# Cross-attention with a feed-forward block: softmax denominators summed on 32 rows of each head and divided chunk by chunk

## The reference, cut to what matters

```python
q, k, v = hidden @ Wq, context @ Wk, context @ Wv      # hidden = layernorm(x)
q, k = layernorm(q, gq, bq), layernorm(k, gk, bk)      # per head of 32
scores = einsum('bhqd,bhkd->bhqk', q, k) / sqrt(32)
attn = softmax(scores, axis=-1)
x = x + einsum('bhqk,bhkd->bhqd', attn, v) @ Wo
s = layernorm(x) @ Win + bin_
h = relu(s[..., None] * W1 + b1)                       # 64 x 16 hidden values
x = x + ((einsum('btmh,mh->btm', h, W2) + b2) @ Wout + bout)
```

## Time and profile before

| | |
|---|---|
| median of three runs | 479.64 us |
| the profiled execution: its time, its span | 481.05 us, 479.2 us |
| busy: TensorE | 433.5 us, 90% |
| VectorE | 358.1 us, 75% |
| ScalarE | 331.6 us, 69% |
| GpSimd | 204.4 us, 43% |
| mean granted TensorE clock | 0.96 of full |
| chain that ended last: TensorE, VectorE, ScalarE | 69%, 15%, 5% |
| one round of the steady part (201.15 to 252.12) | 50.97 us |

### The profile page before, as it was taken

The page is one execution under the profiler, slowest core; times in us unless marked ns, Lnnn a source line. Parts: engine busy times, 40 slices in busy tenths (PEclk is TensorE's granted clock), DMA queues, the critical chain, the costliest instruction groups (busy, mean ns, idle before and its releaser), DMA issues.

```text
span 479.2 us, 7952 instructions
## 1 busy us (share of the span) xinstructions
PE 433.5 (90%) x2456; PEld 279.3 (58%) x2456; DVE 358.1 (75%) x742; ACT 331.6 (69%) x633; POOL 204.4 (43%) x189
## 2 busy tenths in 40 slices
PE   5699888999999999999999999999987998799924
PEld 2386656467376737675667647664653564357712
DVE  4799796687767996799678977695788637537885
ACT  3658747896828983798559856896479639653880
POOL 3326666345514551546253643276342502057300
PEclk9999989999999999999999999999996999799975
DMA  8552685771915187516941493119700690052004
GB/s 306 153 167 68 142 211 138 170 183 33 243 33 126 33 206 168 134 46 156 215 111 28 105 269 67 27 22 234 184 5 0 168 261 16 22 162 80 1 1 175
DMA packets 25290, 58.35 MB, mean 122 GB/s; under 512 B 5921, under 2 KB 6433, under 8 KB 22177
## 3 DMA queue, kind: packets, MB, share of 16 engines
q1 hardware_dynamic: 24992, 57.58, 45.7%
q10 hardware_dynamic: 256, 0.26, 0.2%
HBM read 22.18 MB, written 8.39 MB: 64 GB/s over the span
## 4 chain that ended last, share of the span: by engine, by line
PE 69%; DVE 15%; issue 5%; ACT 5%; SPq 4%; POOL 0%; DMA 0%; DVEq 0%; ACTq 0%; POOLq 0%
PE bank L1929 33%; PE bank L2028 8%; PE bank L1935 7%; PE bank L2016 6%; PE bank L1994 4%; DVE bank L841 4%; PE bank L2096 3%; DVE mx L769 2%; ACT hid L1433 2%; PE bank L2081 2%; PE bank L2031 2%; DVE ssq L757 2%; DVE ln L665 1%; PE bank L2040 1%; PE bank L2003 1%
## 5 line engine op out<-in xcount | busy, mean ns | idle before, releaser
L769 DVE TENSOR_REDUCE mx<-bank 128x4 f32<-128x512 f32 x128 | 83.1, 684 | 22.2 <-PE bank L1994 22.0
L1353 ACT ACTIVATE prob<-bank 128x512 f32<-128x512 f32 x128 | 72.3, 596 | 31.1 <-PE bank L2016 29.1
L520 POOL TENSOR_TENSOR qt_lo<-u,qt_hi 128x512 fp32r<-128x512 f32 x32 | 41.3, 1293 | 70.5 <-ACT u L1330 70.3
L1433 ACT ACTIVATE hid<-s_in,b_col,w_col 128x256 f32<-128x256 f32 x128 | 68.2, 597 | 1.9 <-DVE s_in L821 1.5
L2028 PE MATMUL bank<-prob,v_kv 128*32 128x512 f32 x256 | 66.8, 620 | 0.1
L2031 PE MATMUL bank<-prob,den_sel 128*32 128x512 f32 x256 | 66.3, 621 | 0.0
L841 DVE SCALAR_TENSOR_TENSOR bank<-hid,w_col,bank 128x256 f32<-128x256 f32 x120 | 58.1, 485 | 6.9
L1929 PE MATMUL bank<-wq_hi,zt_hi 128*128 128x512 f32 x128 | 55.3, 432 | 3.0 <-DVE wq_lo L683 3.0
L2016 PE MATMUL bank<-q_stack,k_stack 97*128 97x512 f32 x128 | 50.8, 446 | 7.0 <-DVE att L796 5.9
L513 POOL TENSOR_TENSOR u<-u,lnq 128x512 f32<-128x512 f32 x32 | 32.9, 1050 | 53.8 <-DVE lnq L670 53.8
L525 POOL TENSOR_TENSOR at_lo<-att,at_hi 128x512 fp32r<-128x512 f32 x28 | 35.4, 1281 | 39.3 <-ACT at_hi L1405 39.3
(11 more groups left out here) (158 smaller groups left out, 899.0 us busy)
## 6 DMA issues: line engine op xcount, KB each, us to landing
q_stack<-qt_hi SPq DMA_DIRECT2D x64, 256.0 KB, 4.9
xin<-in_x_dram SPq DMA_DIRECT2D x36, 256.0 KB, 3.9
q_stack<-qt_lo SPq DMA_DIRECT2D x32, 256.0 KB, 4.7
x<-in_x_dram SPq DMA_DIRECT2D x28, 256.0 KB, 4.7
out_dram<-x SPq DMA_DIRECT2D x28, 256.0 KB, 3.3
att<-in_L_xattn_Wk_dram SPq DMA_DIRECT2D x1, 1024.0 KB, 6.5
x<-in_L_xattn_Wq_dram SPq DMA_DIRECT2D x4, 256.0 KB, 7.4
hid<-in_L_xattn_Wv_dram SPq DMA_DIRECT2D x1, 1024.0 KB, 10.2
```

Source lines behind the costliest of these rows:

```text
L520: pool.tensor_tensor(qt_lo[:, :, cols], u[:, j, :].rearrange("p (i n) -> p i n", i=HC), qt_hi[:, :, cols].bitcast(F32), ALU.subtract).then ...
L769: dve.tensor_reduce(mx[:, j, :].rearrange("p (g i) -> p i g", g=G)[:, 2 * half:2 * half + 2, 2 * r:2 * r + 2], maxs_banks[T][half][j][r][: ...
L1353: act.activation(prob[:, h % PR, :], score_bank[t][h][:, :], ACT.Exp, scale=SCALE).then_inc(exp_done, 1)
L1433: act.activation(hid[:, hh % RR, :], of_half(s_in), ACT.Relu, bias=b1_col[:, hh:hh + 1], scale=w1_col[:, hh:hh + 1]).then_inc(hid_done, 1)
```

## The change: what it does

The denominators are summed with a tile of ones of 32 columns, so each head's sum comes out on all of its 32 rows at once, in one bank for each chunk. They are inverted and multiplied chunk by chunk; the spreading matmuls, the split of the inverse, the copy `move_att` and the selectors go. The ring of exponentials has 8 tiles, and `values` and `denominators` take a chunk of four heads each. The Newton step writes back to `rden`, which has two slots.

```diff
-PR = 4
+PR = 8
-        den_sel = sb("den_sel", [P, C, HD])
-        bc_sel = sb("bc_sel", [P, C, P], F32R)
+        ones = sb("ones", [P, HD])
-        rden = sb("rden", [P, TOK])
+        rden = sb("rden", [P, 2, TOK])
...
-            def rden_error(t):
-            def rden_fix(t):
-            def rden_split(t):
+            def rden_error(t, c):
+
+                dve.wait_ge(rden_act, t * C + c + 1)
+                dve.scalar_tensor_tensor(out=den_bank[t][c][:, :], in0=den_bank[t][c][:, :], scalar=-1.0,
+                                         in1=rden[:, c % 2, :], op0=ALU.mult, op1=ALU.mult).then_inc(rden_step, 1)
+
+            def rden_fix(t, c):
+
+                dve.wait_ge(rden_step, t * C + c + 1)
+                dve.scalar_tensor_tensor(out=rden[:, c % 2, :], in0=den_bank[t][c][:, :], scalar=2.0,
+                                         in1=rden[:, c % 2, :], op0=ALU.add, op1=ALU.mult).then_inc(rden_done, 1)
...
+                dve.tensor_tensor(att_of(T)[:, c, :], at_bank[T][c][:, :], rden[:, c % 2, :], ALU.mult).then_inc(att_done, 1)
...
-            def move_att(t, c):
-            def rden_ln(t):
-            def rden_guess(t):
-            def rden_high(t):
+            def rden_ln(t, c):
+
+                act.wait_ge(pv_done, t * PAIRS + 2 * c + 2)
+                if c >= 2 or not first(t):
+                    act.wait_ge(att_done, t * C + c - 1)
+                act.activation(rden[:, c % 2, :], den_bank[t][c][:, :], ACT.Ln).then_inc(rden_log, 1)
+
+            def rden_guess(t, c):
+                act.wait_ge(rden_log, t * C + c + 1)
+                act.activation(rden[:, c % 2, :], rden[:, c % 2, :], ACT.Exp, scale=-1.0).then_inc(rden_act, 1)
...
-            def values(t, pair):
-            def spread(T, c):
+            def values(t, c):
+
+                pe.wait_ge(exp_done, t * H + HC * (c + 1))
...
+                for i in range(HC):
+                    n = HC * c + i
+                    ins = pe.matmul(at_bank[t][c][HD * i:HD * (i + 1), :], v_kv[kv_of(t)][:, n * HD:(n + 1) * HD],
+                                    prob[:, n % PR, :], start=True, stop=True)
                 ins.then_inc(pv_done, 1)
...
+            def denominators(t, c):
+
+                for i in range(HC):
+                    ins = pe.matmul(den_bank[t][c][HD * i:HD * (i + 1), :], ones[:, :], prob[:, (HC * c + i) % PR, :],
+                                    start=True, stop=True)
+                ins.then_inc(pv_done, 1)
```

```diff
+                values(t - 1, 1)
...
+                    pe.wait_ge(out_done, t * 4 - 9)
+                denominators(t - 1, 1)
+                if t >= 3:
+                    pe.wait_ge(out_done, t * 4 - 8)
...
+                max_scores(t, 1, 1)
...
                 scores(t - 1, 8)
...
+                    pe.wait_ge(rden_done, t * 4 - 3)
...
+                max_scores(t, 0, 2)
+                pe.wait_ge(mx_done[1], t * 8 + 3)
                 scores(t - 1, 9)
-                pe.wait_ge(exp_done, t * 16 - 8)
+                pe.wait_ge(exp_done, t * 16 - 7)
                 scores(t - 1, 10)
...
+                pe.wait_ge(mx_done[1], t * 8 + 4)
                 scores(t - 1, 11)
...
+                pe.wait_ge(att_done, t * 4 - 3)
+                turn_z1(t + 2, 0)
...
                 scores(t - 1, 12)
...
+                pe.wait_ge(mx_done[0], t * 8 + 5)
+                scores(t - 1, 13)
                 if t >= 2:
+                    pe.wait_ge(exp_done, t * 16 - 5)
                     project_o(t - 2, 0, 0)
```

More of the change, by code:

```diff
@@ L1080, in epilogue @@
                 add_hidden(3, 15)
-                sum_squares(7, 0)
+                row_max(6, 0, 1, 1)
                 g_low(3)
@@ L1085, in epilogue @@
                 residual2(3, 1)
+                rden_error(5, 0)
+                residual2(3, 3)
+                rden_fix(5, 0)
                 row_max(6, 1, 0, 0)
+                normalise(5, 0)
                 row_max(6, 1, 0, 1)
-                residual2(3, 3)
+                row_max(6, 1, 1, 0)
+                row_max(6, 1, 1, 1)
+                row_max(6, 1, 2, 0)
+                row_max(6, 1, 2, 1)
+                rden_error(5, 1)
+                rden_fix(5, 1)
                 row_max(6, 0, 2, 0)
+                residual1(4, 0)
@@ L1785, in epilogue @@
+                q_high(7, 1)
+                g_high(4)
                 q_high(7, 2)
[L1786 to L1788 removed]
+                exponential(6, 5)
+                q_full(7, 1)
                 q_full(7, 2)
[L1790 to L1791 removed]
+                att_high(5, 0)
+                att_high(5, 1)
+                exponential(6, 6)
+                att_high(5, 2)
+                exponential(6, 7)
@@ new lines, in prologue @@
+                scores(0, 4)
+                pe.wait_ge(zt_lo_done, 12)
+                project_q(2, 3, 0)
+                pe.wait_ge(u_done, 11)
+                pe.wait_ge(exp_done, 1)
+                max_scores(1, 0, 1)
+                project_q(2, 3, 1)
+                pe.wait_ge(exp_done, 4)
+                scores(0, 5)
+                scores(0, 6)
+                pe.wait_ge(qf_done, 8)
+                scores(0, 7)
+                pe.wait_ge(exp_done, 5)
+                values(0, 0)
@@ L2281, in iteration @@
+                max_scores(t, 0, 3)
                 if t >= 2:
@@ new lines, in epilogue @@
+                values(5, 1)
+                pe.wait_ge(exp_done, 89)
+                scores(5, 10)
+                pe.wait_ge(exp_done, 90)
+                denominators(5, 1)
+                pe.wait_ge(rden_done, 21)
+                scores(5, 11)
+                pe.wait_ge(exp_done, 91)
+                pe.wait_ge(out_done, 16)
+                max_scores(6, 1, 1)
+                pe.wait_ge(att_done, 21)
+                scores(5, 12)
+                pe.wait_ge(exp_done, 92)
+                pe.wait_ge(mx_done[1], 49)
@@ new lines, in epilogue @@
+                max_scores(6, 1, 2)
+                pe.wait_ge(mx_done[1], 51)
+                scores(5, 13)
+                pe.wait_ge(exp_done, 93)
+                scores(5, 14)
+                project_o(4, 0, 0)
+                pe.wait_ge(mx_done[1], 52)
+                pe.wait_ge(mx_done[1], 54)
+                max_scores(6, 0, 2)
+                project_o(4, 0, 1)
+                project_o(4, 1, 0)
+                pe.wait_ge(mx_done[0], 53)
+                pe.wait_ge(rden_done, 22)
@@ new lines, in epilogue @@
+                pe.wait_ge(exp_done, 103)
+                values(6, 1)
+                pe.wait_ge(exp_done, 104)
+                pe.wait_ge(mx_done[0], 62)
+                max_scores(7, 1, 1)
+                pe.wait_ge(exp_done, 105)
+                max_scores(7, 1, 2)
+                pe.wait_ge(exp_done, 106)
+                denominators(6, 1)
+                pe.wait_ge(mx_done[1], 59)
+                scores(6, 10)
+                pe.wait_ge(mx_done[1], 60)
+                project_o(5, 0, 0)
```

1637 lines of the change are left out of this document (741 added, 896 removed).

## The result

The changed kernel takes 476.55 us (median of 8 runs, 473.69 to 480.25), beside 479.25 us for the kernel before on the same chip. The ratio is 0.9936, with a 95% interval of 0.991 to 0.9962: faster by 0.6%, where 1.6% was forecast. The profiled execution took 477.64 us, span 475.8 us; for it the forecast was 473.2, so 4.4 us are missing.

A forecast was written before the change was run, and what follows sets the result against it. TensorE was taken to bound the steady rounds, VectorE's add_hidden chain the end. Savings of 3.0 (prologue), 2.0 (filling), 1.4 (steady rounds) and 1.5 (epilogue) made 7.9 us: 473.2 for the profiled execution, 472.0 for the median, range 462 to 484.

The forecast's parts named there:

- TensorE's saving: Each block: four spreading matmuls gone, fewer single pairs and tile-shape changes; 1.37 us of TensorE work less.
- piece (c): From project_y to the first project_o: 9.65 us, 7.1 of work and 2.5 of waiting, where waiting was 1.4.
- Piece (a): From scale_s to g_low: VectorE's about 19.8 us covered by TensorE's some 22 us, though by 2 us or less.
- The lock: VectorE operations with two SBUF inputs and GpSimd SBUF reads exclude each other; in newton1, 0.65 us counted, possibly 1.35 more.
- Prologue, -3.0: Up to 57 us: fold_bias moved later and project_values(0) put into TensorE's wait; 3.0 us less, 5.6 if TensorE bounds.
- Filling, -2.0: From 57 to 150 us: TensorE's saving comes through for the first two blocks, 2 x 1.0 us less.
- Epilogue, -1.5: After 353 us: block 4 net 1.7 us less, block 5 0.5 more; sum 1.2, rounded to 1.5 less.
- F: Follow-up theory, not in the prediction: a TensorE wait costs mostly through the lower clock behind it; epilogue repeats save 1.0 to 1.5 us.
- rival 3: Blocked Newton steps: newton1 takes 2.9 us ahead of residual2, 5.4 us more than the forecast, 477 us; chance 0.10.
- rival 4: Gains hidden: prologue's head start lost in VectorE's row maxima before 98 us, 478 to 479 us; chance 0.10.
- Rival 2: VectorE becomes the bound, from g_low to the first project_o and between the adds: 10 us more, 490; chance 0.15.
- Rival 1: TensorE's whole saving comes through, piece (c) waiting does not grow, prologue gives 5.6 us: 465 us; chance 0.25.

The follow-up runs named there:

- the run with both lists shortened: Changed kernel without chunk 0's Newton step and with ScalarE's logarithm and exp of chunk 1 behind exponential 9: 474.45 us, ratio 0.9892.
- the two kernels shown above: Changed kernel with both maximum_row operations moved back early on ScalarE, 475.88 us; changed kernel with project_values(0) behind project_q(0, 1, 1), 482.13 us.

## Why the prediction was right or wrong

- **The step that failed: every matmul of the steady part and of the filling was taken at its full-clock pitch, and a wait at its own length only. The term for the clock stood at nothing.** Measured, it is 1.5 us a round. TensorE is busy 50.06 us in a round before, 48.17 in the run with both lists shortened (clock 1.00), and 49.65 after: the same work, stretched by 1.48 us behind the waits. It idles 0.91 us before and 1.38 after. Against the kernel before, that is 1.89 us of work less, 0.47 more of idle time, 1.48 for the clock: 0.06 us longer. The forecast had 1.37 less, 1.1 more and nothing for the clock.
- **TensorE's saving, 1.37 us a round: mis-sized, 1.89.** Two full-width pairs do have the pitch of 0.88 us each that I took. Of the difference, 0.36 us are `project_y` (1.49 us to the next matmul, where I took the 1.85 of before): 0.26 of short waits that had counted as work and a change of tile shape. For the four spreads alone the price was too high if one reads it off by adding them (0.47, not 0.94).
- **ScalarE's extra operation "hidden, with 12 us free": this failed too.** Its share of the round is low (39.2 of 51), but in piece (c) its list ends where VectorE's does. I had written that its exponentials reach the point within 0.3 us, and then gave it no price. The runs without the Newton step show it: VectorE 1.1 or 4.0 us lighter, no gain in the rounds.
- **VectorE, 44.6 us a round: 42.8.** The error, fix and multiplication take 0.69, 0.68 and 0.68, as taken. Most of the difference is `newton1`, which lost 1.5 us against the earlier trace rows.
- **Piece (a), covered: right.** For block 4, where I counted 14.1 us from `scale_s` to `g_low`, it is 350.47 to 364.59, 14.12.
- **Piece (c), 9.65 us: 9.70 measured, by luck.** I had 7.1 us of work and 2.5 of waiting. With both lists shortened and the clock held, TensorE's work there is 7.57 us; after has 8.40, so 0.83 is the lower clock, and 1.30 us are idle. And the clock stays low into `project_o`, up to 179.6 us, where I saw no cost at all. Forecast 50.6 a round, measured 51.0.
- **The lock: right in size, and the better half of it missed.** `newton1` takes 1.40 us (forecast 1.6), with one operation of 0.61 us instead of 0.16 that ends within 0.02 us of one on GpSimd; the run with it moved back shows that its place ahead of `residual2` costs almost nothing.
- **Prologue, -3.0: -4.3 at 70 us**, nearly all from `project_values(0)`; `fold_bias` by itself gave nothing at its place. First `project_q` at 22.43 instead of 21.5: VectorE's last `wq_low` ends at 22.33, 0.9 us later than I counted, behind a `key_mean(0)` that now stands ahead of it and takes 1.5 us (16.06 to 17.59).
- **Filling, -2.0: +0.7.** The lead of 4.3 us shrinks to 3.6 at 146.42. At a clock of 1.00 the two kernels shown above gain 1.4 us in this stretch; after's profile, at 0.94 and 0.96, loses that and 0.7 more. It is the same failed step, as far as one execution of each kernel can show it.
- **Epilogue, -1.5: not there.** From 299.83 us to the end only 0.3 us are gained, where 1.85 were forecast with the fourth round. From `project_y` of block 4 to the next `project_o` I had 7.8 us; it took 365.15 to 375.68, 10.5 as before, and TensorE did not idle at all:

```profile
365.15:375.68 10.53, 10.53 (x61) 5.05 (x62) 6.27 (x11) 7.35 (x14) 5.02 (x4) 0.73 0.39 117
```

  I had taken over the lower clock of before as given; here it is 0.73, where this piece had 0.84 before. An estimate from this row, 0.27 of 10.53 us, is that the lower clock takes 2.8 us of it, about what is missing. For the epilogue as a whole this is argued: repeats in two of its waits gave 0.63 us, where F expected 1.0 to 1.5, so part of the cause stays open.

In the sum: 1.4 us are missing at `project_s` of block 0 (3.6 instead of 5.0), 1.5 in the three rounds to 299.83 (+0.5 instead of -1.05), 1.5 behind it. The first (mostly) and the second are the term for the clock that was missing; the third is so in part. (The sum itself gives 471.7 us, 479.64 less 7.9, not 472.0; that is of no weight here.)

**The rivals.** The time is next to rival 3 (477) and rival 4 (478 to 479), but neither mechanism is there: `newton1` lost 0.45 us to GpSimd and not 2.0, and most of the prologue's lead (3.6 of 4.3 us) was still there at 146 us. Rival 2 did not happen. Rival 1's round, 49.6 us, is what the kernel has once its clock is held; its time of 465 assumed the full 5.6 us of the prologue too.

## What to carry to other kernels

Where TensorE is full, a group of short waits can cost the matmuls behind it half their clock, which here was more than the waits themselves; one wait of 0.85 us alone did not the earlier trace rows. Read the pitch of the matmuls behind each wait, not only the wait. Before taking work off the engine that a wait names, look for the other list that releases the next step: here each of the two alone gave nothing, and both, or work put into the wait, gave 1.5 us in 51. Work moved into a wait of the prologue that the profile shows in full (3.04 us) was the safest gain of this change: taken back, it cost by the ratios 4.6 us, more than the whole gain of 2.7 to 3.1.

## What was not expected of the hardware

- Idle time of about 1.3 us in a stretch of 9 to 10 us went with a clock of 0.89 in one kernel and 1.00 in another; the order of the waits differed (1.30 of 9.70, and 1.28 of 8.85).
- The same epilogue instructions took 48.00 us at a mean clock of 0.86 and 45.47 at 0.92, with an edit that ends 80 us ahead of them. The filling stretch of the changed kernel, from 98 us to the first `project_s`, was granted 0.96 in one profile and 1.00 in that of the kernel with `maximum_row` early.
- The kernel before lies between 478.1 and 480.2 us in nearly all of its runs, the changed one between 473.7 and 480.3. Why it varies more is not shown: the kernel with `newton1` moved back has longer waits and lies between 484.9 and 486.8.
